# Attention of a hybrid block: one fp32 exponential per unit, and the product with the values on four 32-column tiles

## The chip, the cores and the metric

One core of a Trainium2 chip. The metric is the device time of one execution in microseconds (us). The core has five engines with queues of their own: TensorE (PE: matrix products into PSUM; its weight loads have their own rows, PEld), VectorE (DVE), ScalarE (ACT), GpSimd (POOL) and SyncE (SP), which issues most transfers. They meet through semaphores.

## The reference

The input is 16 images of 32 x 32 pixels with 32 channels, fp32. Three layers add to it: a filtered activation, attention over the 1,024 pixels of each image, and a routed feed-forward layer. What matters here is the attention:

```
q, k, v = x @ Wq.T, x @ Wk.T, x @ Wv.T          # x: [16, 1024, 32], after a layer norm
scores  = q @ k.T / sqrt(32), causal            # [16, 1024, 1024]
weights = softmax(scores)                       # fp32
out     = weights @ v                           # [16, 1024, 32]
```

## The kernel before

The unit of work is an image ("batch", n = 0 to 15); four make a group (g = 0 to 3). The order of all work is written out by hand: `STEP` (L135 to L148) lists what one step of the outer loop holds, each entry with a shift, so that while image t has its probabilities computed, image t+1 and t+2 have their scores, t+5 and t+4 their two convolutions (`up`, `down`, both L922), and group work (`proj`, `mean`, `dev`, `uT`, `logits`, `select`, `route`, `wT`, `pool`) comes once per four images. `FIRST` and `LAST` are the beginning and the end. Each engine walks through the same list in order and does its own part of every event, so an engine that waits for one event holds back all that follows on it. PSUM is two rings of four banks, psA and psB; PE fills a slot, and a later event that takes the same banks waits until DVE (psA) or ACT (psB) has emptied it.

The probabilities of an image are computed transposed, keys on the partitions, in five units (`PACK`: 1,024 columns in units 0 to 3 and 512 in unit 4). Per unit PE makes the scores (L1035, and the mask, L1038) in psB. ACT then takes the exponential twice from the same PSUM columns, once into the fp32 buffer `e32` (L610) and once into fp16 `Pp` (L611). A third step, the event `low`, subtracts the two and leaves the fp16 rest in the second half of `Pp` (L397): POOL does units 0, 2 and 3, DVE units 1 and 4, and for the last image DVE does all (`pool_takes`, L204). `e32` has three buffers, so ACT waits for the `low` three units back (L602).

The product with the values is the event `pv` (L1039 to L1057), issued in the step after the probabilities, between their unit 0 and unit 1. The values `zV` are fp16 with 64 columns: high parts and low parts of 32 channels side by side. For each of 8 key tiles j and each of the two parts of `Pp`, two matmuls run with 64-column weights, one into PSUM partitions 0 to 63 and one into 64 to 127 (`odd`); together they stream all 128*(8-j) columns. That makes 32 matmuls an image. The result, 512 columns, goes through ACT to `oT` (L615). `proj` (L1058 to L1064) multiplies it in fp32 by `V2`, which adds high and low parts and gives the sums of the probabilities: 8 matmuls with 66 moving columns for two images. DVE divides (L799, L800).

The values reach `zV` by 16 small transfers per image, issued by SP in the event `zK` (L450 to L457) from `z4`, after the fp16 split (`z_split`). In the last image PE runs filler products before each unit of `pv` (L1049, `FILL_PV`: 10 in all, L928).

Of the kernel before, what the change touches and what calls it, by code (L numbers as in the profile page):

```python
# [7 lines left out]
F32 = mybir.dt.float32  # L8
# [7 lines left out]
S = H * W  # L16
# [24 lines left out]
POOL_LOW = (0, 2, 3)  # L41
# [29 lines left out]
C_ID, C_Q, C_QREP, C_MASK, C_AVG, C_BD, C_BDE, C_HALF, C_SUM, C_ROW, C_COLS = 0, 128, 256, 384, 512, 640, 644, 648, 650, 652, 653  # L71

def constants():
# [16 lines left out]
    t[:, C_HALF:C_HALF + 2] = np.kron(np.eye(2), np.ones((2 * C, 1)))  # L91
    t[C - 1::C, C_SUM:C_SUM + 2] = np.kron(np.eye(2), np.ones((2, 1)))
# [4 lines left out]
def batch(ahead, name, *more):  # L97

    return lambda t: (name, t + ahead) + more if 0 <= t + ahead < B else None
# [13 lines left out]
def span_of(n, i):  # L113
# [23 lines left out]
        batch(0, "prob", 1), group(4, "proj", 1), batch(1, "score", 0), batch(0, "low", 0), group(6, "select"),  # L137
# [4 lines left out]
        once(1, "normalise", 2), once(-3, "xT", 2), batch(0, "low", 1), once(2, "gn_var", 3), once(14, "w1", 1),  # L142
        batch(4, "down"), once(-2, "image", 1), batch(0, "low", 2), once(-3, "small", 2),
        batch(0, "prob", 3), once(6, "image_low", 3), group(2, "proj", 0), once(-5, "xT", 1), batch(0, "prob", 4),
        batch(2, "score", 1), once(-4, "small", 1), batch(0, "low", 3), batch(3, "zK"), batch(2, "score", 3),
        group(4, "dev", 1), once(-4, "gn_mean", 1), group(3, "dev", 0), once(-3, "gn_mean", 2), batch(0, "low", 4),
        once(21, "dev", 3, 1), group(6, "route"), once(-3, "normalise", 1), once(-9, "small", 0),
# [53 lines left out]
LOWS = [(n, i) for n in range(B) for i in range(NU)]  # L201

def pool_takes(n, i):  # L204

    return i in POOL_LOW and n < B - 1

def hybrid_kernel(nc, x, bias, up_filter, dn_filter, Wq, Wk, Wv, gate_w, gate_b, weight1, weight2, out):
# [8 lines left out]
    with ExitStack() as ctx:  # L218
# [35 lines left out]
        z32 = sb("z32", [P, KT, C])  # L254
# [12 lines left out]
        rsum = sb("rsum", [P, 3, KT, 2])  # L267
# [25 lines left out]
        V2 = sb("V2", [P, 2 * C + 2])  # L293
# [8 lines left out]
        early = Pp[:, :, :, :].rearrange("p i j n -> p (i j n)").bitcast(F32)  # L302
# [62 lines left out]
        low_by_dve, low_by_pool = sem("low_by_dve"), sem("low_by_pool")  # L365
# [27 lines left out]
        def low_part(queue, engine, n, i):  # L393

            N, o = UCOLS[i], UOFF[i]
            queue.wait_ge(b_drained, BU["prob", n, i] + 1)
            return engine.tensor_tensor(Pp[:, n % 2, 1, o:o + N], e32[:, (NU * n + i) % 3, 0:N], Pp[:, n % 2, 0, o:o + N], ALU.subtract)  # L397

# [13 lines left out]

        def low_count(n, i):

            mine = [m for m in LOWS[:NU * n + i + 1] if pool_takes(*m) == pool_takes(n, i)]
            return (low_by_pool if pool_takes(n, i) else low_by_dve), len(mine)
# [4 lines left out]
        def _(sp):  # L421
# [20 lines left out]
            for e in EVENTS:  # L442
# [41 lines left out]
        def _(pool):  # L484
# [5 lines left out]
            nc.gpsimd.memset(z32[:, :, :], 1.0).then_inc(fills_ready, 1)  # L490
# [16 lines left out]
            for e in EVENTS:  # L507
# [10 lines left out]
                elif name == "low" and pool_takes(*e[1:]):  # L518
                    low_part(pool, nc.gpsimd, g, e[2]).then_inc(low_by_pool, 1)
# [23 lines left out]
        def _(act):  # L543
# [20 lines left out]
            for e in EVENTS:  # L564
# [84 lines left out]
        def _(dve):  # L649
# [19 lines left out]
            for e in EVENTS:  # L669
# [60 lines left out]
                elif name == "small" and n == 1:  # L730
                    link(nc.vector.tensor_copy(T1[:, :, :], s[0:C, 0:C].unsqueeze(1).broadcast_to([C, R, C])))
                    link(nc.vector.tensor_copy(V2[:, 2 * C:2 * C + 2], cst[:, C_SUM:C_SUM + 2]))
                    nc.vector.tensor_tensor(V2[:, 0:2 * C].rearrange("p (b c) -> p b c", b=2), s[:, BANK:BANK + C].unsqueeze(1).broadcast_to([P, 2, C]),
                                            blocks(2, C, P, C_HALF), ALU.mult).then_inc(a_drained, 1)
# [25 lines left out]
                elif name == "split_z":  # L760
# [6 lines left out]
                    nc.vector.tensor_tensor(z32[:, :, 0:C - 1], s[:, :, 0:C - 1],  # L767
                                            zrstd[:, :].unsqueeze(2).broadcast_to([P, KT, C - 1]), ALU.mult).then_inc(z_scaled, 1)
                    dve.wait_ge(z_scaled, n + 1)
                    link(nc.vector.tensor_copy(z4[:, n % 2, :, 0, :], z32[:, :, :]))  # L770
                    nc.vector.tensor_tensor(z4[:, n % 2, :, 1, :], z32[:, :, :], z4[:, n % 2, :, 0, :], ALU.subtract).then_inc(z_split, 1)  # L771
# [17 lines left out]
                elif name == "low" and not pool_takes(*e[1:]):  # L789
                    low_part(dve, nc.vector, n, e[2]).then_inc(low_by_dve, 1)  # L790
                elif name == "proj":
                    if n >= 1:
                        dve.wait_ge(b_filled, BU["logits", n - 1] + 1)
                    first, last = span_of(*e[1:])
                    tiles = KT // 2 * (last - first)
                    sv = s.rearrange("p (k d) -> p k d", k=KT)[:, 0:tiles]
                    av = att[:, BC * first:BC * last].rearrange("p (k d) -> p k d", k=tiles).rearrange("p k (r c) -> p k r c", r=2)
                    inverse_sum = rsum[:, e[2], 0:tiles, :]
                    link(nc.vector.reciprocal(inverse_sum, sv[:, :, 2 * C:2 * C + 2]))  # L799
                    nc.vector.tensor_tensor(av, sv[:, :, 0:2 * C].rearrange("p k (r c) -> p k r c", r=2),  # L800
                                            inverse_sum.unsqueeze(3).broadcast_to([P, tiles, 2, C]), ALU.mult).then_inc(a_drained, 1)
# [101 lines left out]
        def _(pe):  # L903
# [37 lines left out]
            for e in EVENTS:  # L941
# [97 lines left out]
                elif name == "pv":  # L1039
# [93 lines left out]
```

## Time and profile before

| | us |
|---|---|
| median of 3 runs (399.6 to 402.35) | 401.95 |
| the profiled execution, its own time | 401.74 |
| its span, first to last instruction | 399.8 |

Busy in the span: PE 338.4, PE weight loads 254.7, DVE 313.1, ACT 249.8, POOL 239.5. In the page's rows a line `L397 POOL ... x45 | 107.4, 2397` means 45 instructions of that line on that engine, 107.4 us busy in all, 2,397 ns each on average; what follows a second bar is idle time of the engine just before them and who ended it.
### The profile page before, as it was taken

The numbers are of one execution on the slowest core, as the hardware profiler recorded it, in microseconds if no ns is written. First come the engines' busy times: TensorE is split into PE (matmuls) and PEld (weight loads), VectorE is DVE, ScalarE is ACT, GpSimd is POOL, SyncE is SP. The second block draws the span as 40 slices with busy tenths as digits, with TensorE's granted clock in tenths as the row PEclk, the third lists the DMA queues.
The fourth block names the chain that finished last, engine by engine and source line by source line (L and its number), as shares of the span: only waits on it lengthen the run. The fifth ranks groups of instructions, "written<-read, shape, count | busy, mean of one in ns | idle before, by whom it ended". The sixth has DMA issues, their size and how long they took to land.

```text
span 399.8 us, 7830 instructions
## 1 busy us (share of the span) xinstructions
PE 338.4 (85%) x2918; PEld 254.7 (64%) x2918; DVE 313.1 (78%) x558; ACT 249.8 (62%) x331; POOL 239.5 (60%) x141
## 2 busy tenths in 40 slices
PE   1299998899899999989599999998995785968775
PEld 1188867568587686848377768586762443546575
DVE  3677979687969978799759896987989998865521
ACT  1032452797977959698476698788586859731500
POOL 5134454386678898778635989856697936162000
PEclk9999999999999999999799999999998989999655
DMA  4810000000000000000000000000030000001211
GB/s 138 173 25 1 10 14 6 13 13 7 14 5 12 7 9 10 7 11 6 12 3 2 14 7 12 7 8 13 2 61 10 13 0 19 26 0 28 80 52 52
DMA packets 36674, 9.04 MB, mean 23 GB/s; under 512 B 27247, under 2 KB 36509, under 8 KB 36637
## 3 DMA queue, kind: packets, MB, share of 16 engines
q1 hardware_dynamic: 33920, 7.90, 9.1%
q10 hardware_dynamic: 2717, 0.66, 1.2%
q8 instruction: 23, 0.38, 0.4%
q14 instruction: 14, 0.11, 0.1%
HBM read 3.63 MB, written 2.11 MB: 14 GB/s over the span
## 4 chain that ended last, share of the span: by engine, by line
PE 52%; DVE 21%; ACT 8%; POOL 7%; issue 6%; DMA 4%; ACTq 1%; POOLq 0%; SPq 0%; DVEq 0%
PE psB L922 10%; PE psA L922 9%; PE psA L1020 5%; PE psB L1035 4%; DVE negmax L780 4%; PE psB L1056 4%; PE psA L1102 4%; DVE Pp L397 3%; ACT Pp L611 3%; PE psA L1064 3%; PE psA L1080 2%; PE psA L912 2%; POOL urstd L495 2%; PE psB L1071 2%; ACT e L610 2%
## 5 line engine op out<-in xcount | busy, mean ns | idle before, releaser
L397 POOL TENSOR_TENSOR Pp<-e,Pp 128x1024 f16<-128x1024 f32 x45 | 107.4, 2397 | 12.7 <-ACT Pp L611 12.7
L780 DVE TENSOR_REDUCE negmax<-psA 128x1 f32<-128x512 f32 (+7 forms) x128 | 90.5, 748 | 15.6 <-PE psA L1023 14.8
L610 ACT ACTIVATE e<-psB 128x1024 f32<-128x1024 f32 (+1 forms) x80 | 75.7, 946 | 23.6 <-PE psB L1038 15.3
L611 ACT ACTIVATE Pp<-psB 128x1024 f16<-128x1024 f32 (+1 forms) x80 | 75.9, 949 | 0.0
L1020 PE MATMUL psA<-zK,yQ 128*128 128x512 f16 (+1 forms) x192 | 50.4, 346 | 13.9 <-DVE uT L800 5.3
L922 PE MATMUL psB<-xin,UU 128*128 128x224 f16 (+1 forms) x480 | 55.9, 275 | 0.1
L922 PE MATMUL psA<-y,DD 128*128 128x224 f16 (+1 forms) x480 | 55.1, 273 | 0.0
L1035 PE MATMUL psB<-yQ,zK 128*128 128x512 f16 (+1 forms) x192 | 47.7, 331 | 7.0 <-ACT Pp L611 4.5
L922 PEld LDWEIGHTS psB<-xin,UU 128*128 128x128 f16 x480 | 46.8, 99 | 7.7 <-DVE xin L722 0.5
L922 PEld LDWEIGHTS psA<-y,DD 128*128 128x128 f16 x480 | 46.8, 98 | 5.4
L495 POOL TENSOR_TENSOR zrstd<-zrstd,power 128x8 f32<-128x8 f32 x16 | 26.3, 1644 | 29.9 <-DVE zrstd L759 29.6
L517 POOL TENSOR_TENSOR y<-y 128x1024 f16<-128x1024 f32 x16 | 36.6, 2285 | 9.2 <-ACT y L580 9.2
L397 DVE TENSOR_TENSOR Pp<-e,Pp 128x1024 f16<-128x1024 f32 (+1 forms) x35 | 41.0, 1176 | 1.0 <-ACT Pp L611 1.0
L577 ACT ACTIVATE y<-psB 128x1024 f16<-128x1024 f32 x16 | 16.4, 1024 | 36.4 <-PE psB L922 36.4
L1056 PE MATMUL psB<-Pp,zV 128*64 128x128 f16 (+7 forms) x512 | 35.4, 288 | 3.2 <-POOL Pp L397 1.7
L1056 PEld LDWEIGHTS psB<-Pp,zV 128*64 128x64 f16 x512 | 24.2, 110 | 19.2 <-ACT centred L589 4.1
L1020 PEld LDWEIGHTS psA<-zK,yQ 128*128 128x128 f16 x192 | 17.1, 103 | 21.5 <-DVE uT L800 6.3
L495 POOL TENSOR_TENSOR urstd<-urstd,power 128x16 f32<-128x16 f32 (+1 forms) x9 | 26.2, 2916 | 7.6 <-DVE urstd L826 6.9
L1035 PEld LDWEIGHTS psB<-yQ,zK 128*128 128x128 f16 x192 | 17.1, 100 | 20.1 <-ACT Pp L611 6.0
L1038 PE MATMUL psB<-ident_b,mask_b 128*128 128x128 bf16 x128 | 28.2, 220 | 0.0
L525 POOL COPY z<-z 128x512 f16<-128x512 f16 x16 | 9.8, 611 | 30.4 <-DVE z L771 30.4
L1023 PE MATMUL psA<-mask_b,ident_b 128*128 128x128 bf16 x128 | 26.9, 229 | 0.0
(161 smaller groups left out, 584.8 us busy)
## 6 DMA issues: line engine op xcount, KB each, us to landing
zV<-z SPq DMA_DIRECT2D x256, 8.0 KB, 1.8
x_all<-in_x_dram SPq DMA_DIRECT2D x4, 512.0 KB, 4.1
out_dram<-x_all SPq DMA_DIRECT2D x8, 256.0 KB, 2.3
yQ<-rows SPq DMA_DIRECT2D x32, 2.0 KB
Pp<-filter_tables ACTq DMA_DIRECT2D x4, 121.9 KB, 4.3
w_halves<-y SPq DMA_DIRECT2D x12, 32.0 KB, 1.8
cst<-shape_constants SPq DMA_DIRECT2D x1, 326.5 KB, 4.2
y<-in_L_ffn_weight_dram SPq DMA_DIRECT2D x4, 64.0 KB, 2.0
```

Source lines behind the costliest of these rows:

```text
L397: return engine.tensor_tensor(Pp[:, n % 2, 1, o:o + N], e32[:, (NU * n + i) % 3, 0:N], Pp[:, n % 2, 0, o:o + N], ALU.subtract)
L495: return nc.gpsimd.tensor_tensor(v, v, power[:, 0:1].broadcast_to([P, n]), ALU.pow)
L517: nc.gpsimd.tensor_tensor(low, y32[:, :], high, ALU.subtract).then_inc(y_ready, 1)
L610: nc.scalar.activation(e32[:, m % 3, 0:N], slot(e)[:, 0:N], ACT.Exp)
L611: nc.scalar.activation(Pp[:, n % 2, 0, UOFF[e[2]]:UOFF[e[2]] + N], slot(e)[:, 0:N], ACT.Exp).then_inc(b_drained, 1)
L780: ins = nc.vector.tensor_reduce(negmax[:, n % 2, m - 1:m], s[:, at:at + P * m], X, ALU.max, negate=True)
L922: ins = nc.tensor.matmul(within(out_cols, -shift), m, within(v, shift), start=i == 0, stop=i == len(matrices) - 1)
L1020: ins = nc.tensor.matmul(s[:, lo:hi], yQ[:, n % 3, P * (m - 1):P * m], zK[:, n % 3, lo - at:hi - at], start=True, stop=not diagonal)
L1023: ins = nc.tensor.matmul(s[:, hi - P:hi], ident_b[:, :], mask_b[:, :], start=False, stop=True)
L1035: ins = nc.tensor.matmul(s[:, lo:hi], zK[:, n % 3, P * j:P * j + P], yQ[:, n % 3, P * j + lo - at:P * j + hi - at], start=True, stop=not d ...
L1038: ins = nc.tensor.matmul(s[:, lo:lo + P], mask_b[:, :], ident_b[:, :], start=False, stop=True)
L1056: ins = nc.tensor.matmul(rows, zV[:, n % HOMES, j, :], probs_j[:, :, :, C * odd:C * odd + C], start=j == 0 and part == 0, stop=j == KT - 1 ...
```

## The change

Probabilities go to `Pp` in fp32 by one exponential per unit; `e32`, the second exponential, the event `low` and its semaphores are gone. The values `zV` are fp32 with 32 columns, moved from `z32` (now two buffers) instead of `z4`, after `z_scaled` instead of `z_split`. `pv` has four fp32 matmuls per key tile j, each with the same 32-column weights and each into its own 32 PSUM partitions, with a quarter of the columns. Its result is 256 columns. `proj` has 4 matmuls with 132 moving columns for two images.

```diff
-POOL_LOW = (0, 2, 3)
...
-    t[:, C_HALF:C_HALF + 2] = np.kron(np.eye(2), np.ones((2 * C, 1)))
-    t[C - 1::C, C_SUM:C_SUM + 2] = np.kron(np.eye(2), np.ones((2, 1)))
+    t[C - 1::C, C_SUM:C_SUM + R] = np.eye(R)
...
-        batch(0, "prob", 1), group(4, "proj", 1), batch(1, "score", 0), batch(0, "low", 0), group(6, "select"),
+        batch(0, "prob", 1), group(4, "proj", 1), batch(1, "score", 0), group(6, "select"),
...
-        z32 = sb("z32", [P, KT, C])
+        z32 = sb("z32", [P, 2, KT, C])
-        zV = sb("zV", [P, HOMES, KT, 2 * C], F16)
+        zV = sb("zV", [P, HOMES, KT, C])
-        e32 = sb("e32", [P, 3, SLOT])
-        Pp = sb("Pp", [P, 2, 2, PCOLS], F16)
-        oT = sb("oT", [P, GB, BANK])
+        Pp = sb("Pp", [P, 2, PCOLS])
+        oT = sb("oT", [P, GB, BC])
...
-                    sp.wait_ge(z_split, g + 1)
+                    sp.wait_ge(z_scaled, g + 1)
...
                             sp.dma_start(zV[C * r:C * r + C, g % HOMES, i::R, :],
-                                         z4[C * i:C * i + C, g % 2, r::R, 0:2, :].rearrange("p a h c -> p a (h c)")).then_inc(zV_loaded[g % HOMES], 16)
+                                         z32[C * i:C * i + C, g % 2, r::R, :]).then_inc(zV_loaded[g % HOMES], 16)
...
-                elif name == "low" and pool_takes(*e[1:]):
-                    low_part(pool, nc.gpsimd, g, e[2]).then_inc(low_by_pool, 1)
...
-                    m = NU * n + e[2]
-                    if m >= 3:
-                        act.wait_ge(*low_count((m - 3) // NU, (m - 3) % NU))
...
-                    nc.scalar.activation(e32[:, m % 3, 0:N], slot(e)[:, 0:N], ACT.Exp)
-                    nc.scalar.activation(Pp[:, n % 2, 0, UOFF[e[2]]:UOFF[e[2]] + N], slot(e)[:, 0:N], ACT.Exp).then_inc(b_drained, 1)
+                    nc.scalar.activation(Pp[:, n % 2, UOFF[e[2]]:UOFF[e[2]] + N], slot(e)[:, 0:N], ACT.Exp).then_inc(b_drained, 1)
...
-                    nc.scalar.activation(oT[:, n % GB, :], slot(e), ACT.Copy).then_inc(b_drained, 1)
+                    nc.scalar.activation(oT[:, n % GB, :], slot(e)[:, 0:BC], ACT.Copy).then_inc(b_drained, 1)
...
-                elif name == "low" and not pool_takes(*e[1:]):
-                    low_part(dve, nc.vector, n, e[2]).then_inc(low_by_dve, 1)
...
-                            pe.wait_ge(*low_count(n, unit))
+                            pe.wait_ge(b_drained, BU["prob", n, unit] + 1)
                         o, N = PLACE[j], P * (KT - j)
-                        for part in range(2):
-                            probs_j = Pp[:, n % 2, part, o:o + N].rearrange("p (t r q) -> p t r q", r=2, q=2 * C)
-                            for odd in range(2):
-                                rows = s[2 * C * odd:2 * C * odd + 2 * C, :].rearrange("p (r t q) -> p t r q", r=2, t=KT)[:, j:KT]
-                                ins = nc.tensor.matmul(rows, zV[:, n % HOMES, j, :], probs_j[:, :, :, C * odd:C * odd + C],
-                                                       start=j == 0 and part == 0, stop=j == KT - 1 and part == 1, skip_group_check=True)
+                        probs_j = Pp[:, n % 2, o:o + N].rearrange("p (t r q) -> p t r q", r=R, q=C)
+                        for r in range(R):
+                            rows = s[C * r:C * r + C, 0:BC].rearrange("p (t q) -> p t q", t=KT)[:, j:KT]
+                            ins = nc.tensor.matmul(rows, zV[:, n % HOMES, j, :], probs_j[:, :, r, :], start=j == 0, stop=j == KT - 1,
+                                                   skip_group_check=True)
...
-                    for k in range(KT // 2 * (last - first)):
-                        b, a, r = k // 4, k // 2 % 2, k % 2
-                        at = S // 4 * r + P * a
-                        ins = nc.tensor.matmul(s[:, P * k:P * k + 2 * C + 2], oT[:, first + b, at:at + P], V2[:, :], start=True, stop=True)
+                    for k in range(2 * (last - first)):
+                        b, a = k // 2, k % 2
+                        ins = nc.tensor.matmul(s[:, BC * k:BC * k + P + R], oT[:, first + b, P * a:P * a + P], V2[:, :], start=True, stop=True)
```

## Rows read from the trace of the kernel before

**Rows 1.** Busy time, share of the span and instructions of each engine, from the page.

```profile
PE 338.4 (85%) x2918; PEld 254.7 (64%) x2918; DVE 313.1 (78%) x558; ACT 249.8 (62%) x331; POOL 239.5 (60%) x141
```

**Rows 2.** Busy us (instructions) of PE, PEld, DVE, ACT, POOL in four stretches.

```profile
88.00:311.00 223.00, 204.08 (x1864) 153.10 (x1860) 191.48 (x312) 170.80 (x228) 170.50 (x93) 0.98 0.07 11
311.00:353.00 42.00, 32.34 (x273) 18.93 (x272) 36.59 (x53) 31.72 (x39) 21.18 (x11) 0.96 0.06 13
70.00:88.00 18.00, 15.50 (x131) 11.07 (x130) 13.34 (x22) 14.53 (x21) 10.11 (x6) 1.00 0.08 12
353.00:400.00 47.00, 35.12 (x236) 28.35 (x230) 20.52 (x47) 9.79 (x14) 7.82 (x6) 0.70 0.16 45
```

**Rows 3.** The chain that ended last, share of the span by engine.

```profile
PE 52%; DVE 21%; ACT 8%; POOL 7%; issue 6%; DMA 4%; ACTq 1%; POOLq 0%; SPq 0%; DVEq 0%
```

**Rows 4.** The same columns as Rows 2, a full step and the fullest group step.

```profile
105.50:122.70 17.20, 17.20 (x169) 13.61 (x171) 13.89 (x23) 14.86 (x21) 12.48 (x10) 1.00 0.06 10
180.00:202.00 22.00, 17.48 (x130) 13.56 (x132) 19.70 (x28) 13.46 (x20) 14.52 (x8) 0.84 0.06 9
```

**Rows 5.** Groups of instructions by line and shape: low parts, exponentials, result copy.

```profile
L397 POOL TENSOR_TENSOR Pp<-e,Pp 128x1024 f16<-128x1024 f32 x45 | 107.4, 2397 | 12.7 <-ACT Pp L611 12.7
L397 DVE TENSOR_TENSOR Pp<-e,Pp 128x1024 f16<-128x1024 f32 x19 | 25.0, 1323 | 0.0
L397 DVE TENSOR_TENSOR Pp<-e,Pp 128x512 f16<-128x512 f32 x16 | 16.0, 1002 | 1.0 <-ACT Pp L611 1.0
L610 ACT ACTIVATE e<-psB 128x1024 f32<-128x1024 f32 x64 | 66.1, 1033 | 18.3 <-PE psB L1038 15.3 <-PE psB L1035 2.7
L615 ACT ACTIVATE oT<-psB 128x512 f32<-128x512 f32 x16 | 9.9, 618 | 4.1 <-PE psB L1056 4.1
```

**Rows 6.** Busy us (instructions) of L397 alone, DVE then POOL, in two stretches.

```profile
88.00:311.00 223.00, 27.27 (x23) 85.84 (x36) 0.98 0.07 11
311.00:353.00 42.00, 10.95 (x10) 14.61 (x7) 0.96 0.06 13
```

**Rows 7.** What PE's idle time before the scores (L1020) ended on, 88 to 311.

```profile
  DVE uT L800: 11.6, 5
  DVE tF L752: 5.5, 7
  DVE negmax L780: 3.8, 4
```

**Rows 8.** Timeline (start, us, engine, line) of one product with the values, its opening.

```profile
258.45 0.14 PEld L1056 LDWEIGHTS psB<-Pp,zV 128*64 128x64 f16 x4 [0.42 <-ACT centred L589]
258.45 0.41 PE L1056 MATMUL psB<-Pp,zV 128*64 128x512 f16 x2
258.45 0.62 PE L1056 MATMUL psB<-Pp,zV 128*64 128x512 f16 x4
```

**Rows 9.** The chain in order of time (start, us, what): `proj`, `logits` and `pv`.

```profile
224.43 1.97 PE psA L1064 x16
...
254.37 1.86 PE psB L1071 x4
...
258.52 2.08 PE psB L1056 x32
```

**Rows 10.** Timeline: two fp32 matmul records in a row, and the next two.

```profile
254.78 1.02 PE L1071 MATMUL psB<-uT,gateT 128*64 128x512 f32 x2
255.21 1.02 PE L1071 MATMUL psB<-uT,gateT 128*64 128x512 f32 x2
```

**Rows 11.** The chain: fp32 matmuls with 32-column weights, in a stretch at half clock.

```profile
389.36 1.85 PE psA L1093 x32
```

**Rows 12.** Timeline: two low parts on POOL and the matmuls that wait for them.

```profile
334.56 5.41 POOL L397 TENSOR_TENSOR Pp<-e,Pp 128x1024 f16<-128x1024 f32 x2 [3.67 <-ACT Pp L611]
...
340.02 1.02 PE L1056 MATMUL psB<-Pp,zV 128*64 128x320 f16 x20 [1.75 <-POOL Pp L397]
```

**Rows 13.** Timeline: the first filler products inside the last image's `pv`.

```profile
346.94 1.25 PE L928 MATMUL psA<-ident_h 128*128 128x512 f16 x5
```

More of the change, by code:

```diff
@@ L68 @@
 PLACE = {KT - n: UOFF[u] + at for u in range(NU) for n, at in packed(u)}
-C_ID, C_Q, C_QREP, C_MASK, C_AVG, C_BD, C_BDE, C_HALF, C_SUM, C_ROW, C_COLS = 0, 128, 256, 384, 512, 640, 644, 648, 650, 652, 653
+C_ID, C_Q, C_QREP, C_MASK, C_AVG, C_BD, C_BDE, C_SUM, C_ROW, C_COLS = 0, 128, 256, 384, 512, 640, 644, 648, 652, 653
 def constants():
@@ L141 @@
         batch(3, "split_z"), once(-1, "gn_mean", 3), once(-3, "gn_var", 1), once(-5, "dnT", 0), batch(1, "shift"),
-        once(1, "normalise", 2), once(-3, "xT", 2), batch(0, "low", 1), once(2, "gn_var", 3), once(14, "w1", 1),
-        batch(4, "down"), once(-2, "image", 1), batch(0, "low", 2), once(-3, "small", 2),
+        once(1, "normalise", 2), once(-3, "xT", 2), once(2, "gn_var", 3), once(14, "w1", 1),
+        batch(4, "down"), once(-2, "image", 1), once(-3, "small", 2),
         batch(0, "prob", 3), once(6, "image_low", 3), group(2, "proj", 0), once(-5, "xT", 1), batch(0, "prob", 4),
-        batch(2, "score", 1), once(-4, "small", 1), batch(0, "low", 3), batch(3, "zK"), batch(2, "score", 3),
-        group(4, "dev", 1), once(-4, "gn_mean", 1), group(3, "dev", 0), once(-3, "gn_mean", 2), batch(0, "low", 4),
-        once(21, "dev", 3, 1), group(6, "route"), once(-3, "normalise", 1), once(-9, "small", 0),
+        batch(2, "score", 1), once(-4, "small", 1), batch(3, "zK"), batch(2, "score", 3),
+        group(4, "dev", 1), once(-4, "gn_mean", 1), group(3, "dev", 0), once(-3, "gn_mean", 2),         once(21, "dev", 3, 1), group(6, "route"), once(-3, "normalise", 1), once(-9, "small", 0),
         once(17, "proj", 3, 1), group(5, "logits"), batch(4, "tok"), once(5, "normalise", 3), batch(5, "y_low")]
@@ L200 @@
 PLACES = {**place(A), **place(BU)}
-LOWS = [(n, i) for n in range(B) for i in range(NU)]
-def pool_takes(n, i):
-    return i in POOL_LOW and n < B - 1
 def hybrid_kernel(nc, x, bias, up_filter, dn_filter, Wq, Wk, Wv, gate_w, gate_b, weight1, weight2, out):
@@ L266, in hybrid_kernel @@
         att = uT
-        rsum = sb("rsum", [P, 3, KT, 2])
+        rsum = sb("rsum", [P, 3, GB, R])
         nmean = sb("nmean", [P, 3, 2 * KT])
@@ L292, in hybrid_kernel @@
         gateT = sb("gateT", [P, GB, E_])
-        V2 = sb("V2", [P, 2 * C + 2])
+        V2 = sb("V2", [P, P + R])
         Bs = sb("Bs", [P, C])
@@ L300, in hybrid_kernel @@
         obd = sb("obd", [GE, G, GB, C])
-        early = Pp[:, :, :, :].rearrange("p i j n -> p (i j n)").bitcast(F32)
+        early = Pp[:, :, :].rearrange("p i n -> p (i n)")
         def early_part(rows, at, n, a):
@@ L391, in part_of_u @@
             return u[:, :, C * first:C * last].rearrange("p k (b c) -> p b k c", b=last - first)
[L393 to L397, printed above, removed]
         def prob_last(n):
@@ L489, in _ @@
             nc.gpsimd.memset(DD[:, :, :, :, :], 0.0).then_inc(fills_ready, 1)
-            nc.gpsimd.memset(z32[:, :, :], 1.0).then_inc(fills_ready, 1)
+            nc.gpsimd.memset(z32[:, :, :, :], 1.0).then_inc(fills_ready, 1)
             nc.gpsimd.memset(pooled[:, :, :], 1.0).then_inc(fills_ready, 1)
@@ L766, in _ @@
                         dve.wait_ge(*zV_count(n - 2))
-                    nc.vector.tensor_tensor(z32[:, :, 0:C - 1], s[:, :, 0:C - 1],
+                    z = z32[:, n % 2, :, :]
+                    nc.vector.tensor_tensor(z[:, :, 0:C - 1], s[:, :, 0:C - 1],
                                             zrstd[:, :].unsqueeze(2).broadcast_to([P, KT, C - 1]), ALU.mult).then_inc(z_scaled, 1)
                     dve.wait_ge(z_scaled, n + 1)
-                    link(nc.vector.tensor_copy(z4[:, n % 2, :, 0, :], z32[:, :, :]))
-                    nc.vector.tensor_tensor(z4[:, n % 2, :, 1, :], z32[:, :, :], z4[:, n % 2, :, 0, :], ALU.subtract).then_inc(z_split, 1)
+                    link(nc.vector.tensor_copy(z4[:, n % 2, :, 0, :], z))
+                    nc.vector.tensor_tensor(z4[:, n % 2, :, 1, :], z, z4[:, n % 2, :, 0, :], ALU.subtract).then_inc(z_split, 1)
                 elif name == "yQ":
@@ L794, in _ @@
                     first, last = span_of(*e[1:])
-                    tiles = KT // 2 * (last - first)
-                    sv = s.rearrange("p (k d) -> p k d", k=KT)[:, 0:tiles]
-                    av = att[:, BC * first:BC * last].rearrange("p (k d) -> p k d", k=tiles).rearrange("p k (r c) -> p k r c", r=2)
+                    tiles = 2 * (last - first)
+                    sv = s.rearrange("p (k d) -> p k d", k=GB)[:, 0:tiles]
+                    av = att[:, BC * first:BC * last].rearrange("p (k r c) -> p k r c", k=tiles, r=R)
                     inverse_sum = rsum[:, e[2], 0:tiles, :]
-                    link(nc.vector.reciprocal(inverse_sum, sv[:, :, 2 * C:2 * C + 2]))
-                    nc.vector.tensor_tensor(av, sv[:, :, 0:2 * C].rearrange("p k (r c) -> p k r c", r=2),
-                                            inverse_sum.unsqueeze(3).broadcast_to([P, tiles, 2, C]), ALU.mult).then_inc(a_drained, 1)
+                    link(nc.vector.reciprocal(inverse_sum, sv[:, :, P:P + R]))
+                    nc.vector.tensor_tensor(av, sv[:, :, 0:P].rearrange("p k (r c) -> p k r c", r=R),
+                                            inverse_sum.unsqueeze(3).broadcast_to([P, tiles, R, C]), ALU.mult).then_inc(a_drained, 1)
                 elif name == "mean":
```

10 lines of the change are left out of this document (3 added, 7 removed).

## The prediction

> **What bounds the kernel now.** I read the busy times first: PE 338.4 us of 399.8, then DVE with 313.1; ACT and POOL have a third of their time free [rows 1]. The chain of waits agrees: 52% of it is PE, 21% DVE, 8% ACT, 7% POOL [rows 3]. Shares of a whole span mix stages, so the stretches come next. From 88 to 311 us, twelve steps of about 18.6 us, PE is busy 204.08 of 223 us; one plain step is filled to the last (17.20 of 17.20), while in the step heaviest with group work PE has 17.48 of 22 and DVE 19.70 [rows 2, 4]. From 311 to 353, the last four images' attention without convolutions, PE has 32.34 of 42. So PE is the bound in most steps, and its 18.9 us of idle time before 311 stand mostly before the scores, ended by DVE work that came late [rows 7].
>
> The reader should take from this two opposite things. Relief for DVE, ACT and POOL is worth only what PE idles. Any time added to PE in a plain step is paid nearly in full.
>
> **What goes.** The low parts are 107.4 us on POOL and 25.0 + 16.0 us on DVE, the first exponential about 66.1 us (plus the 512-column units) on ACT [rows 5]. Their work is not the bound anywhere for long, so their own price is taken as zero, with PE as the cover; what they give is idle time of PE. In 88 to 311 the visible idle is 18.9 us, and each wait also hides some 0.2 us in which the matmuls before it are still under way, an estimated 8 us for some 40 waits. In that stretch 27.27 us of DVE's 191.48 are low parts [rows 2, 6]; DVE then has 164 of 223, ACT loses a good third. Nothing would come back if the DVE work that ends the waits (division, down copy, row maxima) were late for its own inputs; all 18.9 and some 8 hidden would if every wait were a queue behind low parts. I take 14. From 311 to 353 idle time is 9.7 us; there a POOL low part of 5.41 us for two holds PE back by 1.75 us [rows 12], and ACT's double exponentials hold the scores. Between 0 and 9.7, I take 7, not all, because the last image's ten fillers stay and cost about 0.21 us each whether or not there is a wait to fill [rows 13]. From 70 to 88 it is 2.5 idle, I take 2.
>
> **`proj`.** 16 records in 1.97 us [rows 9] are 0.113 us each once the last one's way out is taken off, with 66 moving columns; the spacing is that of the 128-column fp32 weights. After, there are 8 records with 132 moving columns. By the fp32 rate below they need 0.110, so the same 0.113: 0.9 us less per two images. Six such halves lie in 88 to 311, one in 311 to 353 and one (in two parts) behind: 5.4, 0.9 and 0.9 us. The copy to `oT` has half the columns of 618 ns [rows 5], about 0.2 us less, on the chain once, in the last image.
>
> **`pv`, the term that decides.** Now it is 2.08 us an image [rows 9]. In its rows, two matmuls of 512 columns are under way for the first 0.41 us together, and the next two appear 0.2 us later [rows 8]: the two 64-column tiles stream at the same time, 512 columns in about 0.213 us, and 4,608 column pairs make 1.92 us. The four weight loads of both pairs start within 0.14 us, so loads are pulled ahead of a waiting matmul and hidden.
>
> In fp32 the program's matmul is two records. Two records of 512 columns start at 254.78 and, one later, at 255.21 [rows 10]: 0.43 us for a record, 0.84 ns a column, twice fp16, and a matmul is two records, four times fp16. After the change, key tile j has four matmuls of 32(8-j) columns, eight records. No row shows fp32 matmuls on different column tiles. The bounds are: all four tiles at once, 2 records x 1,152 columns x 0.84 = 1.93 us, as now; and nothing at once, four times that, 7.7 us, plus about 0.2 of issue.
>
> What happens between depends on the order. The queue holds tile 0 first record, tile 0 second record, tile 1 first record, and so on. The second record of tile 0 needs the same tile, so it waits until the first has streamed; if matmuls start in the order of the queue, tile 1 cannot start before it. Then tile 0's second and tile 1's first go together, tile 1's second and tile 2's first, and so on: every matmul costs one record's time, not a half and not two. That is 32 matmuls, 4 x 1,152 columns x 0.84 ns = 3.87 us, plus one short last record and 4 ns for each start, 4.05 us. I take this value: it uses only what the rows show of pairs (they start together when neighbours in the queue have different tiles) and of a tile (the next on the same tile waits). Weight loads don't bound: 32 records with 32-column fp32 weights took 1.85 us at half clock [rows 11], 0.05 each, so 0.03 at full clock, beside record times of 0.21 down to 0.03.
>
> The Trainium skill ("TensorE: Matmul & The Clock Gate", Part 3, What overlaps and what doesn't) says the same of the order: matmuls start and end strictly in program order and only weight loads are moved ahead. Its table of theoretical speedups ("TensorEngine Tiling (Array Packing)", Overview) says up to four times for dimensions of 32 or less; by that alone `pv` would stay at about 2 us. No run here shows either for fp32 tiles.
>
> So `pv` grows by 2.0 us an image: 24 us in 88 to 311 (twelve of them), 8 us behind. It lies on PE, the bound.
>
> **Small edits.** The transfers of the values keep count, size (64 fp16 or 32 fp32 in a piece) and queue, and start two DVE instructions earlier: zero, hidden by the three steps between transfer and use. The wait that replaces `low` in `pv` is for the exponential itself, which is always earlier. The exponential to fp32 takes what the fp16 one takes. One buffer more is cleared at the start: zero. The double buffer of `z32` adds no wait that `z4` did not have.
>
> **The sum**, against the profiled execution's 401.74 us:
>
> - 70 to 88: -2
> - 88 to 311: +24 - 5.4 - 14 = +4.6
> - 311 to 353: +8 - 0.9 - 7 = +0.1
> - end: -0.9 - 0.2 = about -1
>
> Together +1.7, 403.4 us; the median of the runs is 0.2 above the profiled execution. I write 403: PE takes what the others give up.
>
> **The rivals.**
>
> A. Tiles overlap in pairs, waits mostly vanish: 403, as above. Own range 391 to 414: I take back 23 us of 39 (18.9 + 8 + 9.7 + 2.5); the ends are 35 and 12. Chance 0.52.
>
> B. All four tiles stream at once. `pv` stays at 2.08 us, and the gains remain: -2, -5.4 - 10, -0.9 - 5, -1, in all -24 (with less on PE, DVE's own 164 us limit comes nearer, so less idle is taken back): 377. For it: the fp16 pairs do start together, and the load is spread over tiles. Against: two records on one tile stand between the tiles' first ones in the queue. Chance 0.16.
>
> C. fp32 tiles do not overlap at all. `pv` takes 7.9 us, 5.8 more, 93 in all; less 7.2 for `proj` and about 20 of idle: 468. It decides from the point where streaming a 4-byte operand to two tiles is slower than to one; the rows have two 2-byte streams and one 4-byte stream, never two 4-byte ones. Chance 0.12.
>
> D. Pairs as in A, but the idle time stays. The waits of PE end on division, down copy and maxima [rows 7], and if those are late for PE's own matmuls, with PE longer they are later too. Then 32 - 7.2 - 4 (idle of the first and last stretch): about 422. For it: the plain step that has no idle has all its low parts as well [rows 4]. Against: in the heaviest step DVE is nearly full [rows 4] and low parts are in it. Chance 0.14.
>
> The rest, 0.06, is for what I have not seen, on either side.
>
> **The numbers.** This kernel's runs can tell 1% from nothing; that is 398 to 406. Of A, 0.15 lies below, 0.20 within and 0.17 above; B is faster; C and D are slower; the rest splits. Faster 0.33, same 0.22, slower 0.45. The range 376 to 426 holds A and D and most of B and leaves out C.
>
> **What would show it.** One image's `pv` from first to last matmul: 4.05 us (A, D), 2.1 (B), 7.9 (C). In the timeline records start in twos, 0.21 us apart in key tile 0. `proj` at about 1.07 us in 8 records. PE's visible idle time in the twelve steps: about 8 us (A) or some 17 (D). ACT's and POOL's busy time down by 76 and 107, DVE's by 41. I would be wrong most if four-byte streams don't share the array (C), or if the array lets tile 1 pass tile 0's second record (B).

## The result and the profile after

The changed kernel takes 376.19 us (median of 4 runs, 373.74 to 376.78) against 401.8 for the kernel before: a ratio of 0.9375, 95% interval 0.9326 to 0.9424. The forecast of 403 us and its sign were wrong. The time lies just within the low end of the range, but it moved 25 us where I said that it would not move. Rival B had this mechanism, all four column tiles at once, and 377 us.

The page of the changed kernel, busy time and the chain that ended last; they answer to [rows 1, 3].

```profile
PE 331.0 (88%) x3366; PEld 251.1 (67%) x3366; DVE 260.7 (70%) x523; ACT 184.0 (49%) x251; POOL 128.9 (34%) x96
...
PE 73%; DVE 10%; DMA 5%; SPq 4%; issue 3%; ACT 2%; POOL 1%; ACTq 1%; DVEq 0%; POOLq 0%
```

ACT and POOL fell by 66 and 111 us (forecast 76 and 107). ACT's first exponentials were 76 us by themselves, but an exponential starts before the record of the one before it ends (in the kernel before, starts 0.92 us apart for records of 1.03 us), so part of them lay under their neighbours. DVE fell by 52, though the low parts on it were 41 us [rows 5]: other DVE instructions got faster as well. PE is 73% of the chain, before 52%.

The stretches of the changed kernel, columns as in [rows 2]: twelve steps, the last four images, the end.

```profile
88.00:290.00 202.00, 193.43 (x2180) 147.25 (x2176) 154.52 (x287) 121.44 (x168) 83.18 (x57) 0.99 0.08 12
290.00:330.00 40.00, 34.41 (x421) 20.87 (x413) 23.12 (x45) 18.71 (x25) 6.93 (x6) 0.94 0.06 15
330.00:374.00 44.00, 34.38 (x195) 27.14 (x193) 18.53 (x42) 9.01 (x13) 4.10 (x3) 0.61 0.17 48
```

Twelve steps, from one product with the values to the thirteenth, last 202.9 us (86.5 to 289.4) instead of 223.3 (87.8 to 311.1): 20.4 of the 25.4 us by which the span is shorter. Between the two stretches (223 and 202 us) PE's idle time fell from 18.9 [rows 2] to 8.6 us and its busy time by 10.7, of which six shorter division products are 5.0. The gain isn't spread evenly: one step, the heaviest with group work, went from 25.8 (176.1 to 201.9) to 18.2 us.

The opening of one product with the values, from three narrow windows of the timeline (start, us, engine, line, count of records under way); it answers to [rows 8]. A record is one entry of the trace: an fp32 matmul of the program leaves two.

```profile
103.00 0.42 PE L1026 MATMUL psB<-Pp,zV 128*32 128x256 f32 x4
...
103.00 0.64 PE L1026 MATMUL psB<-Pp,zV 128*32 128x256 f32 x8
...
103.00 0.16 PEld L1026 LDWEIGHTS psB<-Pp,zV 128*32 128x32 f32 x8 [0.42 <-issue]
```

Each of the first records lasts 0.40 us. Four take 0.42 us together, so they started within 0.02 us of each other; the next four start 0.24 us after them. The trace doesn't name a record's tile; that these are four tiles is read from the timing, since records on one tile start 0.24 us apart (e10 below). A matmul of the program is two records, so the second record of tile 0 is among the second four, while tile 1's first, behind it in the program, has started already. All eight weight loads lie in the first 0.16 us. The chain of the changed kernel shows the whole product and the product before the division, to compare with [rows 9]:

```profile
206.00 2.10 PE psB L1026 x64
...
208.75 1.09 PE psA L1033 x8
```

2.10 us for 64 fp32 records; it was 2.08 for 32 in fp16.

### The profile page after: what moved, and what is told of

Its sections match the earlier page's. It is cut to its first block, busy times and chain, and to the rows that moved or that the text cites. A ratio compares the mean times of both kernels' runs of the same rounds, so it can differ in the third digit from the quotient of the medians.

```text
span 374.4 us, 8561 instructions
## 1 busy us (share of the span) xinstructions
PE 331.0 (88%) x3366; PEld 251.1 (67%) x3366; DVE 260.7 (70%) x523; ACT 184.0 (49%) x251; POOL 128.9 (34%) x96
## 4 chain that ended last, share of the span: by engine, by line
PE 73%; DVE 10%; DMA 5%; SPq 4%; issue 3%; ACT 2%; POOL 1%; ACTq 1%; DVEq 0%; POOLq 0%
PE psB L893 14%; PE psA L893 12%; PE psB L1026 9%; PE psB L1006 7%; PE psA L991 6%; PE psA L1071 4%; PE psA L883 3%; SPq L434 3%; PE psA L1049 3%; PE psB L1040 2%; DVE negmax L753 2%; PE psA L899 2%; PE psA L984 2%; PE psB L1009 1%; DMA x_all<-in_x_dram 1%
## 5 line engine op out<-in xcount | busy, mean ns | idle before, releaser
L583 ACT ACTIVATE Pp<-psB 128x1024 f32<-128x1024 f32 (+1 forms) x80 | 73.6, 938 | 36.3 <-PE psB L1009 30.7
L991 PE MATMUL psA<-zK,yQ 128*128 128x512 f16 (+1 forms) x192 | 47.4, 329 | 6.0 <-DVE uT L771 2.4
L1026 PE MATMUL psB<-Pp,zV 128*32 128x256 f32 (+7 forms) x1024 | 38.2, 301 | 0.5 <-ACT centred L565 0.4
L1026 PEld LDWEIGHTS psB<-Pp,zV 128*32 128x32 f32 x1024 | 27.8, 114 | 16.0 <-ACT centred L565 4.8
L495 POOL TENSOR_TENSOR y<-y 128x1024 f16<-128x1024 f32 x16 | 34.1, 2132 | 10.2 <-ACT y L556 10.2
L473 POOL TENSOR_TENSOR urstd<-urstd,power 128x16 f32<-128x16 f32 (+1 forms) x9 | 23.6, 2627 | 33.0 <-DVE urstd L797 33.0
L994 PE MATMUL psA<-mask_b,ident_b 128*128 128x128 bf16 x128 | 25.8, 221 | 0.0
L507 POOL TENSOR_TENSOR u<-t_all,nmean 128x512 f32<-128x512 f32 (+1 forms) x8 | 7.9, 993 | 47.0 <-PE psA L1049 29.3
L748 DVE TENSOR_TENSOR yQ<-psA,yQ 64x1024 f16<-64x1024 f32 x16 | 19.6, 1228 | 4.2 <-ACT yQ L574 3.8
L569 ACT ACTIVATE zK<-psB 128x1024 f16<-128x1024 f16 x16 | 16.4, 1027 | 12.1 <-PE psB L978 12.1
```

The lines of the kernel that those rows point to most:

```text
L473: return nc.gpsimd.tensor_tensor(v, v, power[:, 0:1].broadcast_to([P, n]), ALU.pow)
L495: nc.gpsimd.tensor_tensor(low, y32[:, :], high, ALU.subtract).then_inc(y_ready, 1)
L583: nc.scalar.activation(Pp[:, n % 2, UOFF[e[2]]:UOFF[e[2]] + N], slot(e)[:, 0:N], ACT.Exp).then_inc(b_drained, 1)
L748: nc.vector.tensor_tensor(v, s[2 * C:P, :], v, ALU.subtract).then_inc(a_drained, 1)
L991: ins = nc.tensor.matmul(s[:, lo:hi], yQ[:, n % 3, P * (m - 1):P * m], zK[:, n % 3, lo - at:hi - at], start=True, stop=not diagonal)
L994: ins = nc.tensor.matmul(s[:, hi - P:hi], ident_b[:, :], mask_b[:, :], start=False, stop=True)
```

## The experiments

Each run was timed beside the kernel before on its chip; ratios are to that, with 95% intervals. The changed kernel ran once more, beside e4, e5 and e6, as **changed_again**; the absolute times below are held against that run. It spread from 370.35 to 376.26 us over four executions, so a difference of 2 us to it is not a finding. The short diffs give the order of the work, not the words of the program.

> The changed kernel once more, on the chip of the three kernels beside it, so that they can be compared with it directly. All theories: 374 to 378 us.

Measured 374.84 us, 0.9308 [0.9226, 0.9389].

### How records share the array

**e1_same_tile_twice.**

```diff
-for j in range(KT): for r in range(R): matmul(tile r, key tile j)
+for h in range(KT // 2): for r in range(R): for i in range(2): matmul(tile r, key tile 2 * h + i)
```

> The changed kernel, with the product with the values in another order: for two key tiles a and b the matmuls go tile 0 a, tile 0 b, tile 1 a, tile 1 b and so on, so that neighbours in the queue are often on the same column tile. The work is the same. Three theories of how fp32 records share the array. Queue order (the step of the prediction): a record starts only after all before it; then even the changed kernel should not have had four together, and here 3 of 4 record times are serial: about 6.0 us an image for the product, 435 to 440 us in all. Neighbours interleave: the two passes of adjacent matmuls on different tiles go together (first passes, then second passes), but a matmul on the same tile as the one before it ends the set; here the sets are of two, so 3.9 us an image and, with 2 us more on TensorE sixteen times, 400 to 407 us. Own queues: each column tile takes its next record as soon as it is free, past records of other tiles that wait; then 2.0 to 2.2 us an image and 376 to 380 us.

Measured 374.11 us, 0.9309 [0.9261, 0.9357]. The opening of one product, timeline as above:

```profile
102.08 0.44 PE L1025 MATMUL psB<-Pp,zV 128*32 128x256 f32 x4
```

The four take 0.44 us together, so their starts (0, 13, 26 and 40 ns) lie within 0.04 us, though three records for a busy tile stand between neighbours of these four. The fourth has nine records ahead of it in the queue that still wait: three for each of the other tiles. From first to last start the product lasts 2.04 us (1.97 in the changed kernel). Queue order (6.0 us) and interleaved neighbours (3.9) are both out: each tile takes its own next record, also when nine stand before it.

**e7_before_order.** The kernel before, part and half exchanged:

```diff
-for part in range(2): for odd in range(2): matmul(half odd, part)
+for odd in range(2): for part in range(2): matmul(half odd, part)
```

> The kernel before the change, with the two fp16 matmuls of one column half (high and low part) next to each other in the queue instead of alternating halves. Here every record is an instruction of the program. Queue order: the first matmul starts alone, then the second of half 0 and the first of half 1 start together, one record time later (0.21 us for the first key tile); in the long run two still run at once, about 2.2 us an image. Own queues: the first matmul of half 1 starts within 10 ns of the first of half 0, past the waiting second one. The whole time 400 to 404 us either way.

One execution, 402.29 us beside a median of 401.17. Its timeline:

```profile
257.11 0.41 PE L1056 MATMUL psB<-Pp,zV 128*64 128x512 f16 x2
```

Two fp16 matmuls start 7 ns apart although an instruction for half 0 stands between them. So the passing has nothing to do with how fp32 is split into two records: it holds between instructions of the program.

**e10_tile_outer.**

```diff
-for j in range(KT): for r in range(R): matmul(tile r, key tile j)
+for r in range(R): for j in range(KT): matmul(tile r, key tile j)
```

> The changed kernel with the tiles outermost in the product with the values: all eight key tiles on column tile 0, then all on tile 1, and so on. Between the first record of tile 0 and the first of tile 1 stand 15 records with their weight loads, all for a tile that is busy. If own queues reach past all of them: four at a time again, 2.1 to 2.3 us an image and 376 to 380 us. If the array looks only some records ahead, the tiles overlap only at their borders: up to 7.5 us an image and 440 to 465 us; anything between tells how far it looks.

Measured 458.02 us, 1.1407 [1.1336, 1.1478]. The product takes 7.61 us:

```profile
108.44 7.61 PE L1025 MATMUL psB<-Pp,zV 128*32 128x256 f32 x64
```

So there is an end to the passing. At the border between tile 0 and tile 1, the groups of records under way at 110.26 us, and from the groups by shape:

```profile
L1025 PE MATMUL psB<-Pp,zV 128*32 128x256 f32 x1 | 0.4, 403 | 0.0
L1025 PE MATMUL psB<-Pp,zV 128*32 128x96 f32 x2 | 0.3, 246 | 0.0
L1025 PE MATMUL psB<-Pp,zV 128*32 128x64 f32 x1 | 0.2, 219 | 0.0
```

And all that starts or is under way from there to 110.5, of the same line (lowest/median/highest ns, then shapes):

```profile
L1025 PE MATMUL psB<-Pp,zV x7: 193/219/403, 110.1 to 110.4; 128*32 128x96 f32 x2, 128*32 128x64 f32 x2, 128*32 128x32 f32 x2, 128*32 128x256 f32 x1
```

The one with 256 columns is tile 1's first. When it starts, one record of 64 columns and two of 32 are still to come for tile 0: three. So three records of one tile may stand waiting, and the fourth holds up the queue: tile 1's first starts 6 ns after tile 0's fourth from last, and the other two borders of this product look the same. The count goes by tile and not by the whole queue, because in e1 nine were passed, three of each of three tiles. Four for one tile were not tested by themselves.

**e2_two_tiles.**

```diff
-for j in range(KT): for r in range(R): matmul(tile r, key tile j)
+for h in range(2): for j in range(KT): for i in range(2): matmul(tile 2 * h + i, key tile j)
```

> The changed kernel with the product with the values in two halves: first tiles 0 and 1 alternate over all key tiles, then tiles 2 and 3. All theories of sharing give two records at a time, 3.9 us an image, which is what the prediction had taken for the change. So this run sets the prediction's price for the product into the real kernel. If the rest of the sum was right (relief worth 23 us, division products 7), it gives 400 to 407 us. If the relief was worth much more than I took, it gives below 396. The increase over the changed kernel, 16 times 1.95 us, is 31 us if all of it is paid; less if TensorE still idles.

Measured 398.91 us, 0.9944 [0.9915, 0.9973]; the product lasts 3.98 us:

```profile
104.19 3.98 PE L1025 MATMUL psB<-Pp,zV 128*32 128x256 f32 x64
```

This is the kernel that I had forecast, on the chip: 399 where the sum says 403. Its 1.82 us more per image, 29 in all, cost 23 to 25 us. In the twelve steps it is 19.3 of 21.8 us (222.2 against 202.9). The rest of the sum was close in total; the term for the product was the error.

### What the relief was worth

**e3_proj_halves.**

```diff
-matmul(s[:, BC * k:BC * k + P + R], oT[...], V2[:, :])
+for h in (0, 66): matmul(s[:, BC * k + h:BC * k + h + 66], oT[...], V2[:, h:h + 66])
```

> The changed kernel with each product before the division split into two of 66 columns, so that 8 instead of 4 fp32 matmuls do the work of two images, as before the change. TensorE gets its 0.9 us per two images back, 7.2 us in all. Paid in full if TensorE is the bound in all steps: 383 us. If the steps with this product have idle time, 378 to 381.

Measured 374.78 us, 0.9321 [0.9282, 0.9361]: no loss that can be seen beside 374.84. Six of these products lie in the twelve steps and lengthen each by 0.84 us; the steps last 206.2 instead of 202.9 us, the part before them is shorter by 0.8 and the part behind them by 2.0. Behind them TensorE's clock is at half (1.2 GHz) for a shorter time: the mean granted clock between 290 and 361 us is 0.86, in the changed kernel 0.81. I expected 0.9 us each in full; 0.55 is paid in the steps, and the total hides it.

**e4_all_back.**

```diff
+nc.scalar.activation(e16[:, m % 3, 0:N], slot(e)[:, 0:N], ACT.Exp)      # second exponential
 nc.scalar.activation(Pp[...], slot(e)[:, 0:N], ACT.Exp).then_inc(b_drained, 1)
+engine.tensor_tensor(low16[:, m % 3, 0:N], Pp[unit], e16[:, m % 3, 0:N], ALU.subtract)   # event low
```

> The changed kernel with all the removed work of the other engines put back and its waits with it: a second exponential per unit (to fp16) and the subtraction of the two (the low part, to a buffer that nothing reads), by the same engines, at the same places, waited for by the product with the values as before. The product itself stays on four fp32 tiles and the product before the division stays at 4 matmuls. If the whole gain came from relieving ScalarE, VectorE and GpSimd but for the division product, this gives 394 to 398 us. If the gain came from TensorE's shorter work (7 us) in the main, 390 at most would not be reached: 377 to 384.

The waits for the low parts are back as well. Measured 399.74 us, 0.9951 [0.9919, 0.9982]. Against changed_again it is 24.9 us. So nearly the whole gain is the relief of the three other engines. What is left to all other parts of the change, the shorter division product among them, is 1.4 us (401.09 to 399.74; by the interval 0.7 to 3.2); its twelve steps last 223.9 us, no less than the 223.3 of the kernel before.

**e6_exp_back.** The first added line of the diff above alone.

> The changed kernel with the second exponential alone put back, first in order as it was, to a buffer that nothing reads; no subtraction and no wait for one. ScalarE's 76 us are back and each PSUM slot of probabilities is held twice as long. If ScalarE only waits anyway: 375 to 379 us. If the longer slots hold TensorE in every step (0.77 us before the scores in most steps of the kernel before): 384 to 390.

Measured 382.22 us, 0.9537 [0.948, 0.9593]: 7.4 us. It lies between the two forecasts and decides for neither.

**e5_low_back.** The subtraction without the second exponential.

> As the kernel before in this list, but without the second exponential: the subtraction takes a buffer of zeros in its place. So only the work of VectorE and GpSimd and its waits are back (107 us and 41 us). If these two carry the gain: 388 to 396 us. If ScalarE's second exponential and the slots it held in PSUM carried it: 377 to 382.

Measured 407.74 us, 1.0144 [1.0064, 1.0224]: slower than with more work, and outside both forecasts. It has one instruction that the others don't have, a fill of 2.65 us on GpSimd at the start. The first of the twelve steps is 23.6 us instead of 17.6 in e4: TensorE waits 5.6 us there for a VectorE instruction, and its granted clock is 0.86. Over the whole run the granted clock is 0.905 against 0.935 in e4. Why it came so, I did not settle, and I don't use this run for a price.

**e15_pool_low** and **e16_dve_low.** e4 with the subtractions of one engine only:

```diff
+def has_low(n, i): return i in POOL_LOW and n < B - 1          # e15
+def has_low(n, i): return not (i in POOL_LOW and n < B - 1)    # e16
```

> The changed kernel with the second exponential and only GpSimd's subtractions (units 0, 2 and 3 but for the last image, 107 us) put back, with their waits. With the exponential alone it was 382.2 us, with all subtractions 399.7. If GpSimd's part carries the 17.5 us between: 394 to 400. If VectorE's part does: 382 to 386.

> The changed kernel with the second exponential and only VectorE's subtractions (units 1 and 4, and all of the last image, about 41 us) put back, with their waits. If VectorE's part carries the 17.5 us between 382.2 and 399.7: 394 to 400. If GpSimd's does: 383 to 386. If the two halves each give a part, or only both together slow VectorE (its instructions took longer while GpSimd worked: 2,397 ns of work each beside it): both runs near 388.

Measured 385.18 us, 0.9596 [0.9548, 0.9645], and 387.12 us, 0.9656 [0.9601, 0.971]: 3.0 and 4.9 us over the exponential alone, together (e4) 17.5. e15 fits its second forecast, 382 to 386; e16 comes near the third of its own, both runs near 388. The parts don't add up: 3.0 + 4.9 is less than half. Busy times with the exponential alone (e6), then with GpSimd's part (e15):

```profile
PE 328.6 (86%) x3366; PEld 249.2 (66%) x3366; DVE 258.9 (68%) x523; ACT 246.1 (65%) x331; POOL 128.1 (34%) x96
```

```profile
PE 332.7 (86%) x3366; PEld 251.3 (65%) x3366; DVE 271.7 (71%) x523; ACT 246.7 (64%) x331; POOL 223.2 (58%) x141
```

In e15 DVE has not one instruction more than in e6 and is busy for 12.8 us more. One of its small instructions, the scaling of 16 means, shows how; GpSimd's subtraction and this instruction in the timeline of e15:

```profile
144.76 2.13 POOL L402 TENSOR_TENSOR low<-Pp,e 128x1024 f16<-128x1024 f32 x1
145.35 1.58 DVE L819 TENSOR_SCALAR nmean<-nmean 128x16 f32<-128x16 f32 x1
```

It takes 0.17 us in five of its seven executions, and 1.58 us in the two that start while a subtraction runs on GpSimd; it then ends 0.03 us after that subtraction. In the kernel before it is 1.27 and 1.58 us in two of seven, in the changed kernel 0.17 in all. So it does not run slower, it waits. Record by record, 9.2 of the 12.8 us lie in 16 DVE instructions that overlap a GpSimd subtraction; the other 113 that overlap one are not lengthened by more than 0.05 us. It depends on the instruction and on when it comes: in e4, with all subtractions back, the scaling of 16 means met none and took 0.17 us each time.

The subtractions wait for each other in the same way. GpSimd's in e15, and VectorE's 512-column ones in e16, where each is alone:

```profile
L402 POOL TENSOR_TENSOR low<-Pp,e 128x1024 f16<-128x1024 f32 x45 | 96.0, 2137 | 18.0 <-ACT Pp L617 17.9
```

```profile
L402 DVE TENSOR_TENSOR low<-Pp,e 128x512 f16<-128x512 f32 x16 | 10.9, 682 | 1.0 <-ACT Pp L617 1.0
```

Both together in e4:

```profile
L397 POOL TENSOR_TENSOR low<-Pp,e 128x1024 f16<-128x1024 f32 x45 | 108.1, 2410 | 11.5 <-ACT Pp L611 11.5
L397 DVE TENSOR_TENSOR low<-Pp,e 128x512 f16<-128x512 f32 x16 | 17.7, 1105 | 1.0 <-ACT Pp L611 1.0
```

The means are 2,410 against 2,137 ns on GpSimd and 1,105 against 682 ns on VectorE, but they mix two kinds: in e4, ten of VectorE's 16 take 0.68 us as when alone and the six others 1.5 to 2.0, and of GpSimd's 45 most take 2.13 us, ten take 3.1 and some lie between.

That these waits are what makes 17.5 us out of 3.0 and 4.9 is argued and not shown. A part may be the clock: in the stretch from 88 to 290 us its granted mean is 1.00 in e6, 0.99 in e15 and e16, and 0.97 in e4.

### Short fp32 products on column tiles elsewhere

**e12_pool_tiles.**

```diff
-    matmul(s[:, 0:GE], u[:, k, :], wT[:, k, :], start=k == 0, stop=k == KT - 1)
+    for b in range(GB):
+        matmul(s[C * b:C * b + C, E_ * b:E_ * b + E_], u[:, k, C * b:C * b + C], wT[:, k, E_ * b:E_ * b + E_],
+               start=k == 0, stop=k == KT - 1, skip_group_check=True)
```

> The changed kernel with the pooling product (8 fp32 matmuls a group with 128-column weights and 64 moving columns, 1.9 us, of which only four diagonal blocks are read) as 32 matmuls on four column tiles, each with 32-column weights and the 16 columns of its own block. If fp32 tiles run at once and weight loads of 32 columns take a quarter of those of 128: 0.5 to 0.8 us a group, so 1.1 to 1.4 us less on TensorE three times at full clock and 2 to 2.5 us once at half clock, at the end, where it is on the chain: 370 to 373 us, if changed_again is 375. If short matmuls are bound by how fast they are handed on: no gain, 375.

Measured 368.85 us, 0.9171 [0.9124, 0.9219]. The last group's product in the chain of the changed kernel and of this one, both at half clock (granted 0.50):

```profile
357.77 3.62 PE psA L1049 x16
```

```profile
352.97 1.03 PE psA L1050 x64
```

The three others, at full clock, went from 1.69 to 0.54 us from first to last start.

**e17_before_pool_tiles.** The same edit in the kernel before.

> The kernel before with its pooling product on four column tiles, as in the run pool_tiles. TensorE's time falls by 1.3 us three times within the steps and by 2.6 us once at the end, where nothing covers it. If TensorE is the bound in the steps of the kernel before, as the prediction read it: 6 us less, 395 to 396. If its steps are set by chains through VectorE and GpSimd: only the end, 398 to 400.

Measured 397.07 us, 0.9886 [0.9841, 0.9931]: 4.3 us, between the two forecasts; the interval (395.0 to 398.6 us) reaches into both. Its twelve steps are 2.4 us shorter, as much as the two products in them.

**e14_pool_logits.** e12, and

```diff
-matmul(s[0:GE, BANK * i:BANK * i + BANK], gateT[:, :, :], uT[:, BANK * i:BANK * i + BANK])
+matmul(s[GE * i:GE * i + GE, 0:BANK], gateT[:, :, :], uT[:, BANK * i:BANK * i + BANK])
```

ScalarE empties the two halves in two instructions instead of one.

> The changed kernel with the pooling product on four tiles and the gate logits on two: the two fp32 matmuls of 512 columns with 64-column weights go to the two column halves and run together, 0.9 us less a group at full clock, 1.7 us less in the last group at half clock; ScalarE empties the two halves in two instructions (0.25 us more). If TensorE binds the steps: 2.7 us there and 1.5 at the end, 364 to 366 us against 369. If only the end is exposed: 367 to 368.

Measured 365.56 us, 0.9105 [0.9046, 0.9163], 3.3 us less than e12. This is the fastest version found, against 0.9375 for the change itself: the same trick in two more places.

**e13_pool_tiles_no_fill.** e12 with `FILL_PV = (0, 0, 0, 0, 0)`.

> The changed kernel with the pooling product on four tiles and without the ten filler products in the last image's product with the values. They take 2.1 us on the chain now that nothing has to be waited for there. If the clock stays as granted: 366 to 367 us. If TensorE's clock falls earlier for want of them: 369 to 372.

Measured 367.71 us, 0.9173 [0.9102, 0.9244]: the same as e12 (0.9171). The fillers can go or stay.

## Why the prediction was wrong

**The step that failed** is in the part on `pv`: "The second record of tile 0 needs the same tile, so it waits until the first has streamed; if matmuls start in the order of the queue, tile 1 cannot start before it." The first half holds, the condition does not. The rows that I had showed neighbours on different tiles only, and could not tell order in the queue from order per tile. I took order because it needed the least. The term was 4.05 us an image; it measured 2.10, and e1, e7 and e10 show why: a record waits for its own tile and passes those that wait for others, up to three of one tile (e10) and nine in all (e1). Put into the kernel, the forecast product (e2, 3.98 us) gives 398.91 us, so this one term was worth 23 to 25 us.

The Trainium skill ("TensorE: Matmul & The Clock Gate", Part 3, What overlaps and what doesn't) says that matmuls start and end strictly in program order. For starts the traces disagree, in fp32 (three records passed in the changed kernel, nine in e1, by the fourth tile's first) and in fp16 (one passed in e7); the measurement decides. The Trainium skill ("TensorEngine Tiling (Array Packing)", Overview) gives up to four times for dimensions of 32 or less. The traces agree: 64 records of 32 to 256 columns in 2.10 us, and 7.61 us with the tiles outermost (e10), 3.6 times.

**The bounds and rates held.** 0.84 ns a column for a record [rows 10], 1.93 us for four at once, 7.7 for none: measured 1.97 from first to last start, and 7.41 with the tiles outermost. The weight loads are hidden: the 1.97 us are within 0.04 of what the columns alone give.

**The division product** was sized right as work (1.07 us forecast, 1.09 measured) and wrong as gain. I booked 7.2 us as paid in full. e4 against the kernel before shows 1.4 us, e3 against the changed kernel 3.3 us of 5.0 in the steps and nothing in the total. "Any time added to PE in a plain step is paid nearly in full" holds for the product with the values (19.3 of 21.8 us in the steps of e2) and for the pooling product (e12 takes 2.0 us off the steps and e17 2.4, for 2.3 of shorter products), and only in part for this one.

**The relief** I put at 23 us in A and 17 in B. e4 gives 24.9 with the short product. That B's 377 is so near is luck: two errors cancelled, about 6 us for `proj` too much and 8 for relief too little. What I left out is that the removed work also held up what stayed. DVE went down by 52 us, not 41: the 272.1 us that it had beside the subtractions became 260.7. e15 shows where it comes from: with GpSimd's subtractions alone back, DVE's unchanged instructions are busy for 12.8 us more. How many of the 24.9 us hang on this, no run shows. The Trainium skill ("SBUF — State Buffer", section SBUF: two separate sides) describes one port pair that the two engines share: an instruction of VectorE in a two-port mode or with two inputs in SBUF, and one of GpSimd, lock it in turn, and the one that comes second waits until the first is done. The traces agree: the scaling of means takes 1.58 us instead of 0.17 and ends 0.03 us after GpSimd's subtraction. I should have read it as a rule that bears on this change.

**A reading that was too large.** The 11.6, 5.5 and 3.8 us of [rows 7] make 20.9 us, more than the 18.9 that PE idles in all: they count the wait of a matmul and that of its weight load, which is mostly the same time. For the matmuls alone the same stretch has

```profile
PE psA L1020 <- DVE uT L800: 5.3, 2, 4.5
```

and 2.4 and 1.6 us for the two others. So about half of PE's idle time stood before these scores, and not most of it; 3.6 us were a wait for GpSimd.

**Rival D** (idle time stays) is out: 8.6 us remain of 18.9, as A had it ("about 8"). **Rival C** did not come; two and four 4-byte streams ran at once without loss.

**What stays open:** why the low parts without the second exponential (e5) are slower than with it, and why the two halves of the low parts cost 7.9 us one by one and 17.5 together; and how much of the 6.0 us that e12 gains comes from shorter products and how much from the clock at the end. The four products are shorter by 1.1 us three times and by 2.6 once, which would be all of it, but the kernels also differ in which stretches near the end run at half clock.

## What to carry to other kernels

A small fp32 product need not be split into fp16 parts by other engines: on four 32-column tiles it costs what the fp16 parts on two 64-column tiles did, if neighbours in the queue lie on different tiles, or at most four records in a row are for one tile (e1; with 16 in a row it was 7.6 us instead of 2.1). Look for other products of which only diagonal blocks are read, and for two short ones with 64-column weights: there the same move gave 9.3 us more (374.84 to 365.56). And when work leaves GpSimd, count what it did to VectorE's other instructions, not only its own time: look for one whose longest execution ends with a GpSimd instruction, since a mean hides it.

## What the runs showed that was not expected

- A matmul passes records that wait for other column tiles, up to three of one tile: four start within 0.02 us with one between each (changed kernel) and within 0.04 with three between each (e1), where the fourth passes nine. With fifteen between, tiles overlap only at their border and the product takes 7.6 us.
- VectorE's and GpSimd's subtractions of 682 and 2,137 ns have means of 1,105 and 2,410 ns together, because some wait for the other engine (up to 1,981 and 3,117 ns) and most don't.
- Costs of freed engines don't add: 7.4, 3.0 and 4.9 us (e6, and e15 and e16 beside e6) make 15.3, all together cost 24.9 (e4).
- 64 fp32 records with 32-column weights and 16 moving columns take 1.03 us at half clock, 16 ns each; 16 with 128-column weights and 64 columns took 3.62.
